# Delta-rule heads: the key projection, two of its taps, the weight turns and the second merge level are placed and built otherwise

## The reference, cut to what matters

```python
q = causal_conv_silu(x @ Wq.T); k = causal_conv_silu(x @ Wk.T)   # four taps each
v = causal_conv_silu(x @ Wv.T); beta = sigmoid(x @ Wb.T)
g = exp(-exp(A_log) * softplus(x @ Wa.T + dt_bias))
q, k = l2norm(q), l2norm(k)                                      # per head
def step(S, (q_t, k_t, v_t, g_t, beta_t)):
    error = v_t - g_t * (S.T @ k_t)
    S = g_t * S + outer(k_t, beta_t * error)
    return S, S.T @ q_t
o = scan(step)
o = rmsnorm(o) * norm_w * silu(x @ Wg.T)
return o @ Wo.T
```

## Time and profile before

| | us |
|---|---|
| median of three runs | 3418.72 |
| the profiled execution | 3415.16 |
| its span | 3413.4 |
| busy TensorE / DVE / ACT / POOL | 3180.1 / 2191.9 / 1898.9 / 1672.6 |
| delta heads, 158 to 1600 us: TensorE / DVE / ACT / POOL | 1421.4 / 1049.8 / 1034.5 / 1138.9 |
| matmuls and weight loads of the whole program | 18834 each |

### The profile page before, as it was taken

The page is one execution under the profiler, slowest core; times in us unless marked ns, Lnnn a source line. Parts: engine busy times, 40 slices in busy tenths (PEclk is TensorE's granted clock), DMA queues, the critical chain, the costliest instruction groups (busy, mean ns, idle before and its releaser), DMA issues. The chain is left out here.

```text
span 3413.4 us, 60026 instructions
## 1 busy us (share of the span) xinstructions
PE 3180.1 (93%) x18834; PEld 2544.9 (75%) x18834; DVE 2191.9 (64%) x4849; ACT 1898.9 (56%) x4657; POOL 1672.6 (49%) x3107
## 2 busy tenths in 40 slices
PE   6899999999999999999999788799979999998998
PEld 3688888888888888888878555488866777776543
DVE  5577777777777777777653488765547567574432
ACT  3677777777777777777532377644445445363111
POOL 2777787777788777778630000145534002011322
PEclk9899999999999999999999999999989999999999
DMA  4222222222222222222353333423351222211854
GB/s 113 63 73 69 59 69 62 73 68 67 74 55 73 62 73 68 65 76 53 97 176 92 115 142 142 177 87 103 115 174 57 68 69 69 93 65 53 271 99 56
DMA packets 432408, 310.47 MB, mean 91 GB/s; under 512 B 130496, under 2 KB 347456, under 8 KB 431072
## 3 DMA queue, kind: packets, MB, share of 16 engines
q1 hardware_dynamic: 423792, 289.57, 28.8%
q0 software_dynamic: 8432, 18.88, 2.8%
HBM read 177.97 MB, written 130.43 MB: 90 GB/s over the span
## 5 line engine op out<-in xcount | busy, mean ns | idle before, releaser
L631 PE MATMUL gd_PJ<-xn_lead,gd_w_rest 128*128 128x512 f32 x1024 | 421.3, 411 | 0.5 <-DVE gd_w_rest L786 0.5
L631 PE MATMUL gd_PJ<-xn_lead,gd_w_lead 128*128 128x512 f32 x1024 | 403.0, 394 | 0.0
L631 PE MATMUL gd_PJ<-xn_rest,gd_w_lead 128*128 128x512 f32 x1024 | 401.9, 393 | 0.0
L1079 POOL TENSOR_TENSOR gd_prod<-gd_L,gd_T 32x14 f32<-32x14 f32 (+6 forms) x896 | 324.8, 362 | 70.4
L1082 POOL TENSOR_TENSOR gd_T<-gd_T,gd_prod 32x14 f32<-32x14 f32 (+6 forms) x896 | 311.6, 348 | 71.6 <-POOL gd_prod L1079 2.5
L793 DVE SCALAR_TENSOR_TENSOR gd_conv<-gd_pre,gd_cur_a,gd_conv 128x512 f32<-128x512 f32 x384 | 301.8, 786 | 13.3 <-ACT gd_conv L958 2.9
L631 PEld LDWEIGHTS gd_PJ<-xn_lead,gd_w_lead 128*128 128x128 f32 x1024 | 193.8, 189 | 43.4
L631 PEld LDWEIGHTS gd_PJ<-xn_lead,gd_w_rest 128*128 128x128 f32 x1024 | 194.4, 190 | 38.5 <-DVE gd_w_rest L786 0.9
L631 PEld LDWEIGHTS gd_PJ<-xn_rest,gd_w_lead 128*128 128x128 f32 x1024 | 194.6, 190 | 35.3
L932 DVE SCALAR_TENSOR_TENSOR gd_og<-gd_B,ptab,gd_gate 128x512 f32<-128x512 f32 x64 | 48.1, 751 | 243.8 <-PE gd_B L645 243.8
L2619 ACT ACTIVATE sa_E<-sa_B,sa_nmax 128x512 f32<-128x512 f32 (+3 forms) x256 | 131.3, 525 | 131.4 <-DVE sa_nmax L2756 127.2
(11 more groups left out here) (476 smaller groups left out, 8620.3 us busy)
## 6 DMA issues: line engine op xcount, KB each, us to landing
expert_rows<-xt_blank SPq DMA_DIRECT2D x16, 2112.0 KB, 7.3
turned_queries_keys<-f_wq SPq DMA_DIRECT2D x16, 1280.0 KB, 6.0
x_wo<-decay_sums SPq DMA_DIRECT2D x64, 256.0 KB, 3.7
triangles<-gd_Lo SPq DMA_DIRECT2D x64, 256.0 KB, 3.5
gd_W<-turned_image SPq DMA_DIRECT2D x64, 256.0 KB
gd_T<-inverse_image SPq DMA_DIRECT2D x64, 256.0 KB
gated_outputs<-gd_og SPq DMA_DIRECT2D x64, 256.0 KB, 2.8
go_ogt<-gated_outputs SPq DMA_DIRECT2D x16, 1024.0 KB, 5.9
```

Of the source, the lines that this page charges most:

```text
L631: mm = pe.matmul(bank, w_parts[wp][:, j, k, :], rhs, start=(k == 0 and wp == 1), stop=(k == KT - 1 and wp + xp == 0))
L1079: nc.gpsimd.tensor_tensor(prod[:, rows, 0:j], L16[:, rows, j:j + 1].to_broadcast(shape), T16[:, j:j + 1, 0:j].to_broadcast(shape), ALU.mul ...
```

## The change

What it does:

- The k projection (JK) comes before the gate's projection (JG) at the end of TensorE's slot, and ACT copies it in the same slot, ahead of the gate's silu, in place of at the next slot's start. Taps 0 and 1 of k for chunk n+3 run at the end of DVE's slot ahead of the gated output; tap 2 stays at the next slot's start. Their parameters come from a tile of their own, cur_c, which POOL fills for the next head in c=1 behind the solve.
- JK's turn is at the end of c=0, JQ's at the end of c=2 (both ahead of the transposes of o), JV's in c=2 ahead of merge(2). Their banks change (TURN_BANK); ACT's and DVE's parts follow.
- The second merge level (32 to 64) computes only the two blocks that matter, as 32x32 products, with two banks for the two quadrants. `inv` takes the place of T for the later levels. The product is copied into W, not added. It waits for og of the slot before, as Bk[0] is shared with it.
- R is written in place into Vb. On DVE the taps of q come before the k by k diagonal, merged(2) before the four small operations on k's length; on ACT the root of k's length comes behind the silu of q.

```diff
@@ tensor: spread_rows, merge
-                    if l < NM - 1:
+                    if l == 0:
                         each(half[2], tiles(Lo_c), [second(W_c, MERGE[l])[:, b] for b in range(B)], y_sum)
+                    elif l == 1:
+                        pe.wait_ge(og_ready, n + 1)
+                        pe.sem_inc(blocks_open, 1)
+                        for b in range(B):
+                            for q, bank in PAIRS:
+                                lo, hi = slice(q, q + SIDE), slice(q + SIDE, q + 2 * SIDE)
+                                mm = pe.matmul(bank[lo, b, 0:SIDE], Lo_c[hi, b, lo], W_c[hi, b, hi], start=True, stop=True)
+                        mm.then_inc(y_sum, 1)
...
+                    pe.wait_ge(inv_ready, n * (NM - 1) + l)
+                    if l == 1:
+                        pe.sem_inc(blocks_open, 1)
+                        for b in range(B):
+                            for q, bank in UPPERS:
+                                at = slice(q, q + SIDE)
+                                mm = pe.matmul(bank[at, b, 0:SIDE], inv[at, b, q:q + SIDE], Y[at, l % 2, b, 0:SIDE], start=True, stop=True)
+                        mm.then_inc(wup, 1)
@@ tensor: order of the slot
-                if back and more and c == CH - 1:
-                    pe.wait_ge(g_silu, n + 2)
-                    turn_weights(h1, JQ)
...
-                if back and more and c == 1:
-                    pe.wait_ge(k_pre, n + 3)
-                    turn_weights(i + 1, JK)
...
+                if back and more and c == 2:
+                    pe.wait_ge(q_pre, n + 2)
+                    turn_weights(i + 1, JV)
                 if back:
                     merge(2)
...
                     project(JK, c3, k_proj)
+                if has1:
+                    pe.wait_ge(q_pre, n + 2)
+                    if back and more and c == 2:
+                        pe.wait_ge(w_copied, (i + 1) * 4 + JV + 1)
+                    else:
+                        pe.wait_ge(w_copied, h1 * 4 + JG + 1)
+                    project(JG, c1, g_proj)
+                if back and more and c in (0, 2):
+                    pe.wait_ge(k_pre, n + 4)
+                    turn_weights(i + 1, JK if c == 0 else JQ)
                 if back:
                     pe.wait_ge(o_ready, n + 2)
                     turned(Bk[0], tiles(o), o_turned)
@@ vector
+                    if l == 1:
+                        for q, bank in PAIRS:
+                            at = slice(q, q + SIDE)
+                            ts = nc.vector.tensor_scalar(Y[at, l % 2, :, 0:SIDE], bank[at, :, 0:SIDE], -1.0, None, ALU.mult)
+                        ts.then_inc(y_ready, 1)
...
-                    nc.vector.transpose(T_c, W_c).then_inc(t_next, 1)
+                    nc.vector.transpose(inv[0:TOP, :, 0:TOP], W_c[0:TOP, :, 0:TOP])
+                    at = slice(2 * SIDE, 3 * SIDE)
+                    nc.vector.transpose(inv[at, :, at], W_c[at, :, at]).then_inc(inv_ready, 1)
...
-                    tap(n + 2, par, PK, cur_k, (0,), k_tap)
+                    tap(n + 2, par, PK, cur_c, (2,), k_tap)
...
+                if has3:
+                    dve.wait_ge(k_halo, n + 4)
+                    dve.wait_ge(k_pre, n + 4)
+                    tap(n + 3, parm, PK, cur_c, (0, 1), k_tap)
@@ scalar
-                if has2 and (back or c > 2):
-                    act.wait_ge(k_proj, n + 3)
-                    act.wait_ge(head_k, h2 + 1)
-                    copy_pre(par, PK, JK, cur_k, k_pre)
...
+                if has3 and (back or c > 1):
+                    act.wait_ge(k_proj, n + 4)
+                    act.wait_ge(head_c, h3 + 1)
+                    copy_pre(parm, PK, JK, cur_c, k_pre)
                 if has1:
                     act.wait_ge(g_proj, n + 2)
                     nc.scalar.activation(gate[:, parm, :], PJ[:, W_BANK[JG], :], ACT.Silu).then_inc(g_silu, 1)
+                if back and more and c in (0, 2):
+                    lead_weights(i + 1, JK if c == 0 else JQ)
@@ gpsimd
+                if has3 and c == 1 and back:
+                    pool.wait_ge(k_tap, (n + 3) * 3)
+                    row(cur_c, h3, head_c)
```

More of the change, by code:

```diff
@@ L505, in delta_heads @@
         solving, solved, cleared, masks_set = sem("solving"), sem("solved"), sem("cleared"), sem("masks_set")
-        y_sum, y_ready, wup, w_ready, t_next = (sem(x) for x in ("ysum", "y", "wup", "w", "t"))
+        y_sum, y_ready, wup, w_ready, inv_ready, blocks_open = (sem(x) for x in ("ysum", "y", "wup", "w", "inv", "blocks"))
         ks_done, r_ready, oi_sum, oi_ready, u_sum, u_ready, o_sum, o_ready, s_sum, s_ready, sd_ready = (
@@ L672, in merge @@
                         pe.wait_ge(p_ready, n + 1)
-                    else:
[L674 to L678, removed]
-                if back and more and c == CH - 1:
-                    pe.wait_ge(g_silu, n + 2)
-                    turn_weights(h1, JQ)
+                        each(half[3], tiles(T_c), [Y[:, l % 2, b, :] for b in range(B)], wup)
+                        return
+                    pe.wait_ge(inv_ready, n * (NM - 1) + l)
[6 more added lines that the diff above has]
+                        mm.then_inc(wup, 1)
+                    else:
+                        each(half[3][0:TOP], [inv[:, b, 0:TOP] for b in range(B)], [Y[:, l % 2, b, :] for b in range(B)], wup)
                 if back:
@@ L748, in slot @@
                     each(Bk[1], tiles(Kd), tiles(U), s_sum)
-                if back and more and c == 2:
-                    pe.wait_ge(v_pre, n + 4)
-                    turn_weights(i + 1, JV)
                 if has1:
@@ L858, in slot @@
                     tap(n + 1, parm, PQ, cur_a, (0,), q_tap)
-                if back and more and c == 1:
-                    rest_weights(i + 1, JK)
+                if back:
+                    masked(2)
+                if has1:
+                    tap(n + 1, parm, PQ, cur_a, (1, 2), q_tap)
                 if has2:
@@ L869, in slot @@
                 if back:
-                    turned_corner()
-                    masked(2)
-                if has1:
-                    tap(n + 1, parm, PQ, cur_a, (1, 2), q_tap)
+                    merged(2)
                 if has2:
@@ L903, in slot @@
                     nc.vector.tensor_scalar(qss[:, :], qss[:, :], 1e-24, None, ALU.max).then_inc(q_max, 1)
+                if back and more and c == 2:
+                    rest_weights(i + 1, JV)
                 if back:
@@ L920, in slot @@
                         nc.vector.tensor_copy(S[:], Bk[1][:, :, :]).then_inc(s_ready, 1)
-                if back and more and c == 2:
-                    rest_weights(i + 1, JV)
                 if has1:
@@ L986, in slot @@
                     copy_pre(parm, PQ, JQ, cur_a, q_pre)
-                if back and more and c == 1:
-                    lead_weights(i + 1, JK)
-                if has2:
-                    act.wait_ge(k_len, n + 3)
-                    nc.scalar.activation(klen[:, :], kss[:, :], ACT.Sqrt).then_inc(k_root, 1)
                 if back and c > 0:
@@ L1008, in slot @@
                     nc.scalar.copy(U[:], Bk[1][:, :, :]).then_inc(u_ready, 1)
+                if back and more and c == 2:
+                    lead_weights(i + 1, JV)
                 if has1:
@@ L1018, in slot @@
                     silu(PV, vT[:, :], v_silu)
-                if back and more and c == 2:
-                    lead_weights(i + 1, JV)
                 if has3:
@@ L1139, in slot @@
                     nc.gpsimd.tensor_copy(end[:, parm, :], cur_a[:, P_END + c1 * B:P_END + c1 * B + B]).then_inc(extra_done, 1)
+            row(cur_c, 0, head_c)
             row(cur_k, 0, head_k)
```

105 lines of the change are left out of this document (50 added, 55 removed).

## The result

Before: median 3419.6 us (3413.2 to 3421.3, four runs). After: median 3449.9 us (3439.5 to 3454.8, four runs). The ratio is 1.0097, 95% interval 1.0081 to 1.0112: slower by about 1%, 30 us, where 17 us less was forecast. The profiled run of after took 3454.8 us (span 3453.0, mean granted clock 0.972), that of before 3415.2 (3413.4, 0.981), so 39.6 us lie between the two traces. By TensorE's starts, 31.7 of them lie between the first product of the first slot and that of the last; 8.1 come behind. Of these, 5.2 lie behind the heads' last product, where the program is the same in both (1702.8 and 1708.0 us). Over all the traces here that stretch takes 1701.8 to 1709.1 us, so these 5.2 are not put down to the change.

A forecast was written before the change was run, and what follows sets the result against it. TensorE's stream was taken to bound c=1 and c=2, a chain over POOL c=3 and c=0. Slots of 24.21, 25.00 and 49.3 make a head 98.5 against 99.6 us; 3418.7-17.5 = 3401 us, range 3376 to 3430.

The forecast's parts named there:

- Keys ahead of the gate, two taps moved: End of DVE's slot: early k copy, two taps in idle time; 0.33 us saved in c=2, og and masked(0) 0.3-0.5 late in c=0.
- chain-bound part: Slots c=3 and c=0, bound by the chain from qss over POOL to c=1, at least 49.0 us together, whatever TensorE does.
- Pairs: spread_rows(1) and merge(1): 32x32 products at 0.03 us a record, burst 0.71 to 0.73 us, 0.32 less a slot.
- rival A: Pair bursts on TensorE: the two quadrants run side by side, burst 0.48 us, 41 us less, 3378; chance 0.2.
- Rival B: spread_rows(1) and merge(1): 32x32 records no faster than 64-column ones, burst 0.9, 30 us slower, 3449; chance 0.15.
- DVE's side is hidden: Second merge level: DVE's copies for the 32x32 products are ready behind the k by k burst (0.93 us), as the old ones were.
- k's late copy in c=2: ACT's 2.16 us wait for POOL's refill of cur_k goes, and with it TensorE's 0.33 us ahead of merge(1).
- JK's turn: Weight transposes of 0.44 us move from c=1 to the end of c=0, where the stall before c=1 takes them.
- second bound: POOL chain, 30.4 us from qss to c=1; its sign: TensorE waits 0.8 to 1.2 us for the inverse image at c=1.
- c=3 and c=0: These two slots together: qss ends 19.2 us into c=3, plus 30.4, less 0.3 for relief: 49.3 us, from 48.7 to 50.1.
- C: POOL chain takes it all: qss late by 0.95, taps beside POOL stretch both; c=3+c=0 50.0, 3412 us; chance 0.15.
- D: ACT becomes late: sqrt ahead of the copy of v, U behind it, 0.3 us in c=1 and c=2; 3410 us; chance 0.08.

The follow-up runs named there:

- copy_first: The changed kernel with ACT's copy of the projected k ahead of the two exponentials of the decays, not behind them: 3395.9 us, ratio 0.9931 to the kernel before.
- pairs_only: The kernel before with only the second merge level as 32x32 pairs, with inv; no turn, projection or tap moved: 3432.2 us, ratio 1.0043.
- taps_back: The changed kernel with taps 0 and 1 of k again behind masked(0) of the next slot: 3400.7 us, ratio 0.9953 to the kernel before.

## Why the prediction was wrong

- **The step that failed** is "Keys ahead of the gate, two taps moved": that two k taps run at the end of DVE's slot, "where DVE had nothing to do but wait", and that og and masked(0) come 0.3 to 0.5 late only in c=0. The idle stretch was real, 3.56 us ahead of og on DVE before. But I did not ask when the input is there. ACT's copy ends 1.5 us into it, behind two exponentials. Nor does the prediction give the pair a length in that place: it is 1.54 us in idle time (copy_first), two taps at 2.10 beside POOL stood in the earlier trace rows, and it took 3.26. 1.49+3.26 = 4.75 us don't fit into 3.56; and the stretch itself ended up 1.5 us shorter, for DVE's work ahead of it ran later (1.85 us to the slot's start in place of 3.35). Taking the move back turns 1.0097 into 0.9953, making the copy early 0.9931.
- **The last link** was missing too: the time was put "inside the chain-bound part" of c=0 and so costed at nothing. The stall it could hide in is 0.8 us a head; the wait was 2.5 in c=0, 0.7 to 0.8 in c=1 and c=2 and 0.34 in c=3, and behind 2.5 us without work came 1.5 us of lower clock.
- **Pairs**: mis-sized, by 0.34 us a slot to the good. A burst is 0.37 in place of 0.71, because the quadrants overlap; that is rival A, better than the 0.48 it had. Rival B fell: no burst came near 0.9, and that its 3449 us is the time measured is chance. "DVE's side is hidden" held only with the new order; pairs_only shows the level by itself as a loss.
- **Right**: k's late copy in c=2 is gone, and its 0.33. JK's turn leaves c=1. In copy_first, with the taps' start mended, the forecast's terms for c=1 and c=2 hold with the pairs' measured 0.66: 24.97-0.44-0.66 = 23.87 (23.80) and 25.65-0.33-0.66 = 24.66 (24.58). The time is 0.9931 of 3418.7, 3395, where 3401 was forecast. In after no wait for the inverse image is left at c=1; by the prediction's own sign that would refute the second bound, but the longer c=0 only hid it, and copy_first has it back (14.2 us).
- **Right by luck**: c=3 and c=0 were forecast at 49.3 and take 49.42 in copy_first, but by two misses that cancel. qss was predicted 19.2 into c=3 and comes at 20.0 there (in after at 1041.73-1021.51 = 20.2), and the chain behind it takes 29.7 in place of 30.4.
- **C and D** named the right neighbours, taps beside POOL and a late ACT, but looked for the harm in the chain to c=1 and in U. It was ahead of merge(0). JQ's rest weights are late in c=3, 0.45 by the starts, above the 0 to 0.2 allowed; that is part of why qss is late.
- **Open**: lateness and length of the taps are priced apart only in part: with an early start a pair of 2.5 to 3.1 us cost merge(0) nothing at three of four slot ends, but at c=3's end copy_first makes the pair both early and short. The keys ahead of the gate and the turns were not measured singly.

## What to carry to other kernels

Before work is put into idle time of an engine, look up when its inputs are written, what the engine that slows it (here POOL) does in that stretch, and whether the change leaves the stretch as long as it was; the length of the gap alone says nothing. A cut on the bound engine can be lost in the queue of the next one: the pairs lost by themselves (1.0043) and won only beside the moves (0.9953 in taps_back, 0.9931 with the early copy). The moves without pairs ran only with the late copy (1.0162), so what they are worth by themselves isn't shown. A new wait ahead of a dense stretch can cost more than its length, by the lower clock behind it: here one of 2.5 us did in most heads, one of 1.6 in half of them.

## What the runs showed of the hardware

32x32 fp32 products (32 moving columns, two records each) start their records 0.032 us apart in one quadrant, and 0.017 in the mean when two quadrants take turns, side by side. A 128x512 DVE operation with two SBUF inputs goes from 0.75 to 1.59 and 1.64 us beside POOL's wide tensor_tensor, and POOL's from 1.28 to 1.59 and 1.71; with an input in PSUM it stays at 0.74. After 2.50 us in which TensorE had nothing to do, the granted clock was 0.61 over a 4.4 us window that starts 1 us after work resumed. It also fell behind shorter waits, though not each time: to 0.51 behind 1.59 us (pairs_only) and to 0.50 behind waits of 1.14 and 0.68 us, 2.2 us from start to start of the products that waited (taps_back).
